# Routing the first half of the tokens inside attention, and the shared expert in two parts, in a transformer block with experts

## The chip, the cores and the metric

The kernel runs on one core of a Trainium2 chip. A core has a matrix engine (PE, or TensorE, with its weight loads shown as PEld), a vector engine (DVE), a scalar engine for activations (ACT), a general engine (POOL, or GpSimd), and an engine that issues transfers (SP). Each engine works off its own instructions in the order written, and waits at semaphores for the others. The metric is the device time of one execution in microseconds (us), as the median of three runs.

## The reference

Four sequences of 1024 tokens with 128 channels pass attention with 16 heads and then a mixture of experts. Cut to what matters:

```
mod = (silu(c) @ wmod).reshape(4, 6, 1, 128)          # sa, ca, ga, sb, cb, gb
h = layernorm(x) * (1 + ca) + sa
x = x + ga * attention(h)                              # causal, rotary, 16 heads of 8 channels
h = layernorm(x) * (1 + cb) + sb
shared = (silu(h @ sg.T) * (h @ su.T)) @ sd.T          # one shared expert, 352 hidden channels
probs = softmax(h @ wr.T + rb)                         # 7 routed experts
w = the two largest probs of a token, divided by their sum
x = x + gb * (shared + sum_e w[e] * expert_e(h))       # each expert like the shared one
```

## The kernel before

**Units.** The 4096 tokens are 32 tiles of 128, and 8 chunks of 512 tokens (CG = 4 tiles each). A half is 4 chunks, 16 tiles, two sequences (GT, GC, GTILES). Attention goes through 16 groups of four heads of one sequence: groups 0 to 3 are sequence 0, groups 12 to 15 sequence 3. NQ is 16, so NQ - 2 and NQ - 1 are the last two.

**Attention.** A group has ten steps of three slots (lines 67 to 71). In a step PE writes two pairs of score matrices (L1681) into banks 0 to 3, ACT takes the exponentials (L973), POOL masks the steps on the diagonal (L775), and PE multiplies the probabilities of two steps earlier with the values (L1658, function `values_product`) into bank 4. The scores of step s, pair p wait for the exponential of the pair before the last. In the slots between, PE works on a ring of three further banks (5 to 7). What goes through it is written out in a list, `RING_PIECES`, made by `quad_pieces`: row maxima of the next groups (L1602 on PE, L1210, L1238, L1243 on DVE), a "shift" that turns these maxima, which ACT and POOL then split in three parts and SP copies into the next group's operands (`load_shift`), a "norm" (PE turns four tiles of output, DVE divides by the sums, L1260 and L1263), and for finished sequences a "turn" (PE transposes, DVE copies, L1249) and a "project" (PE multiplies with the gated output weights L1627, DVE adds to x L1252 and takes statistics L1124). PE writes an entry when DVE, or ACT for a shift, has taken the entry three earlier; DVE works the entries off in the list's order. So both engines follow the same list, and an entry that waits holds up all that is written behind it on PE, the scores included. The slots of turn and project are computed: in group 14 eight entries from slot 9 on, in group 15 four from slot 2 on. The last group writes no maxima.

**Transition.** After group 15, PE transposes and projects the last sequence (L1710, L1766). DVE finishes the variance of sequences 0 to 2 and then of sequence 3; ACT takes the square roots (L995, `deviation`) and normalises chunk by chunk (L1001, `normalise`); PE transposes the rows (L1722, `turn_normalised`), ACT applies the modulation twice (L1011 in full and L1014 as the high part `h2_hi`, `modulate2`), DVE makes the low part (L1293, `second2`). `router` (L1728) gives the logits, and `softmax_shift`, `softmax_scale`, `ranks`, `weights`, `prefix`, `starts`, `slots` and `experts` on DVE make of them each token's two experts and its places in the sorted order; `counts` are two products on PE (L1736). The shared expert of a chunk is three pieces of six products (L1750, `gate_up`), a silu of each (L1030) and a product on DVE (L1416, `hidden`), and twelve products back (L1758, `down`) that DVE adds to x (L1420). A piece is written when the piece two earlier has been taken. All eight chunks pass here, the routing of both halves on DVE between them. POOL modulates the first half's rows (L789, L793) and scatters them with indirect transfers, one per tile and choice, 32 for a half (L782), into `slot_rows_scratch`, which SP has filled with zeros by one transfer of 5.4 MB issued at the end of group 14. The weights of the seven experts come through two raw buffers: SP loads (L617, L618), ACT makes the high part (L1019, `first_part`), DVE the low part (L1425, `second_part`), and the load of expert e waits for the low part of expert e - 2.

**Routed tiles.** Each half has 38 tiles (STG) of 128 sorted rows of one expert. All 76 follow each other as one pipeline: SP loads the rows (L638, four buffers), PE transposes (L1831), ACT and DVE make high and low parts (L1080, L1525), PE multiplies with gate and up weights (L1843), ACT and DVE make the hidden values (L1087, L1532), PE transposes (L1864) and multiplies back (L1854), ACT weighs (L1096), and POOL scatters the result (L844). In the first 24 tiles POOL also has one scatter of the second half's rows in each. SP reads the first half's results back while tiles of the second run, DVE combines them. At the end the second half's results are read, added by POOL (L861) and DVE (L1541, L1543), and stored.

## Time and profile before

| | |
|---|---|
| median of 3 runs | 799.03 us (798.55 to 799.05) |
| profiled execution | 797.6 us, its span 795.9 us |
| mean granted TensorE clock | 0.947 of full speed |
| PE busy | 686.8 us, 86% of the span |
| DVE busy | 573.4 us, 72% |
| ACT busy | 545.9 us, 69% |
| POOL busy | 342.0 us, 43% |
| chain that ended last, by engine | PE 59%, DVE 18%, ACT 9%, issue 7%, DMA 3% |

The span is cut into stages. Attention runs to 489.7, the transition to the first routed tile at 594.7, the tiles to 772, and the rest is reading back and storing. The share of an engine over the whole span is a mean over these, so the stretches below say more. A row of the timeline gives start, duration, engine, line, operation, what is written and read, how many instructions are merged, and in brackets how long the engine had been idle and what ended that. Durations of neighbours overlap a little: the distance of two starts is what an instruction costs on an engine that is full. `PEclk` is the granted clock, 1.00 for 2.4 GHz and 0.50 for 1.2 GHz.

### The profile page before, as it was taken

Reading aid. Unit: us, or ns where it says so; the run is one execution under the profiler, and the core shown is the slowest. Engines: PE = TensorE matmul, PEld = TensorE weight load, DVE = VectorE, ACT = ScalarE, POOL = GpSimd, SP = SyncE. Lnnn points to the kernel's source line nnn. Section 1 sums busy time; section 2 is a strip of 40 time slices with the busy share of each in tenths; the row PEclk is TensorE's granted clock in tenths of the full one; section 3 lists DMA queues with packets and bytes.
Section 4 is the critical chain, followed back from the end, with each engine's and each line's share of the span. In section 5 each row is a group of like instructions: output and inputs, shape, how many; then the busy total and the mean of one; then the engine's idle time right before and its main releaser. Section 6 shows DMA issues by size and latency. Waiting matters only on the chain.

```text
span 795.9 us, 18082 instructions
## 1 busy us (share of the span) xinstructions
PE 686.8 (86%) x5304; PEld 395.3 (50%) x5304; DVE 573.4 (72%) x2042; ACT 545.9 (69%) x1013; POOL 342.0 (43%) x551
## 2 busy tenths in 40 slices
PE   2986899999999999999999986678869989999970
PEld 1553123333333333333333434567659889999960
DVE  5797889999999999999999834574773323333543
ACT  2785259889989888989888788544325556666640
POOL 1367613232322322232322123235657887666652
PEclk9999569999999999999999999699999999999995
DMA  9246021111111111111110079202233322223425
GB/s 260 83 156 219 1 74 47 39 30 29 47 47 48 47 28 30 41 46 47 48 37 14 1 136 178 68 23 81 63 92 78 82 76 81 66 68 104 131 87 158
DMA packets 64760, 59.46 MB, mean 75 GB/s; under 512 B 10798, under 2 KB 52398, under 8 KB 64668
## 3 DMA queue, kind: packets, MB, share of 16 engines
q1 hardware_dynamic: 58924, 46.85, 23.3%
q0 software_dynamic: 4480, 9.64, 3.4%
q10 hardware_dynamic: 1264, 1.84, 0.7%
q8 instruction: 46, 0.75, 0.4%
q14 instruction: 46, 0.38, 0.2%
HBM read 33.57 MB, written 24.33 MB: 73 GB/s over the span
## 4 chain that ended last, share of the span: by engine, by line
PE 59%; DVE 18%; ACT 9%; issue 7%; DMA 3%; POOL 1%; SPq 1%; ACTq 1%; DVEq 0%; POOLq 0%
PE ps L1658 13%; PE ps L1602 10%; PE ps L1843 9%; PE ps L1681 7%; PE ps L1854 6%; DVE junk L1238 5%; ACT probs L973 5%; PE ps L1864 3%; PE ps L1758 2%; PE ps L1636 2%; DVE junk L1210 2%; PE ps L1750 2%; DMA routed_results_scratch<-y_s,s_dest 1%; PE ps L1831 1%; DVE rot L1193 1%
## 5 line engine op out<-in xcount | busy, mean ns | idle before, releaser
L973 ACT ACTIVATE probs<-ps 128x1024 f32<-128x1024 f32 (+1 forms) x320 | 285.5, 941 | 34.5 <-PE ps L1681 32.1
L1210 DVE CUSTOM_DVE_ANT_0 junk<-ps,tri 128x512 f32<-128x512 f32 (+3 forms) x512 | 218.5, 487 | 13.9 <-PE ps L1602 11.6
L1602 PE MATMUL ps<-ka,qa 61*128 61x256 bf16 (+3 forms) x788 | 186.7, 325 | 10.0 <-DVE rowmax L1210 3.0
L775 POOL TENSOR_SCALAR_AFFINE_SELECT probs<-probs 128x512 f32<-128x512 f32 x128 | 79.7, 634 | 191.8 <-ACT probs L973 191.8
L1658 PE MATMUL ps<-probs,v 128*32 128x512 f32 (+3 forms) x1536 | 157.7, 498 | 1.3 <-POOL probs L775 1.1
L1681 PE MATMUL ps<-qa,ka 64*128 64x512 bf16 (+3 forms) x768 | 144.6, 331 | 7.7 <-ACT probs L973 5.6
L1602 PEld LDWEIGHTS ps<-ka,qa 61*128 61x128 bf16 x788 | 53.0, 95 | 159.8 <-DVE rowmax L1210 80.4
L844 POOL DMA_INDIRECT routed_results_scratch<-y_s,s_dest x76 | 76.2, 1003 | 41.0 <-issue 35.0
L782 POOL DMA_INDIRECT slot_rows_scratch<-rows,slot x64 | 64.1, 1001 | 56.6 <-DVE slot L1393 30.1
L1243 DVE TENSOR_REDUCE leftmax<-ps 128x1 f32<-128x512 f32 x120 | 78.4, 686 | 8.5 <-PE ps L1602 8.5
L1532 DVE TENSOR_TENSOR hid_s<-sg,ps 128x352 f32<-128x352 f32 x76 | 39.6, 521 | 46.2 <-ACT sg L1087 46.0
L1854 PE MATMUL ps<-wd,hidT 128*128 (+1 forms) x456 | 64.3, 277 | 5.8 <-ACT hidT L1105 5.8
L1525 DVE TENSOR_TENSOR h_lo<-ps,h_hi 128x128 fp32r<-128x128 f32 x76 | 22.2, 291 | 59.7 <-ACT h_hi L1080 59.3
L1854 PEld LDWEIGHTS ps<-wd,hidT 128*128 128x128 f32 (+1 forms) x456 | 60.6, 192 | 7.4 <-issue 7.3
L1658 PEld LDWEIGHTS ps<-probs,v 128*32 128x32 f32 x1536 | 33.8, 108 | 54.5 <-issue 49.3
L1681 PEld LDWEIGHTS ps<-qa,ka 64*128 64x128 bf16 x768 | 42.5, 94 | 33.4 <-ACT probs L973 21.2
L1087 ACT ACTIVATE sg<-ps 128x352 f32<-128x352 f32 x76 | 35.2, 463 | 33.8 <-PE ps L1843 32.0
L1096 ACT ACTIVATE y_s<-ps,s_weight 128x128 f32<-128x128 f32 x76 | 27.9, 367 | 33.5 <-PE ps L1854 25.4
L1238 DVE CUSTOM_DVE_ANT_0 junk<-ps,above 128x256 f32<-128x256 f32 x136 | 49.3, 419 | 0.0
L749 POOL TENSOR_TENSOR mrest<-mneg,mparts 32x128 f32<-32x128 f32 x16 | 6.7, 417 | 92.7 <-ACT mparts L936 92.7
L1843 PE MATMUL ps<-w_hi,h_hi 128*128 x152 | 45.3, 380 | 1.2 <-issue 1.1
L1210 DVE DVE_READ_ACCUMULATOR2_ANT rowmax<- 128x1 f32 x512 | 42.6, 83 | 0.1
(195 smaller groups left out, 1168.4 us busy)
## 6 DMA issues: line engine op xcount, KB each, us to landing
slot_rows_scratch<-cst SPq DMA_DIRECT2D x1, 5396.0 KB, 36.1
srow<-slot_rows_scratch SPq DMA_DIRECT2D x76, 71.0 KB
k_parts_scratch<-qk_parts SPq DMA_DIRECT2D x12, 320.0 KB, 2.7
ka<-k_parts_scratch SPq DMA_DIRECT2D x32, 120.0 KB
q_parts_scratch<-qk_parts SPq DMA_DIRECT2D x12, 256.0 KB, 2.6
qa<-q_parts_scratch SPq DMA_DIRECT2D x32, 96.0 KB
ka<-k_parts_scratch SPq DMA_DIRECT2D x32, 80.0 KB
xs<-in_x SPq DMA_DIRECT2D x4, 512.0 KB, 9.4
```

What stands on the lines that cost most here:

```text
L775: nc.gpsimd.affine_select(out=p, in_=p, compare_op=ALU.is_ge, fill=0.0, base=0, pattern=[[0, HQ], [1, T]], channel_multiplier=-1).then_inc ...
L782: nc.gpsimd.indirect_dma_start(slot_d, bass.IndirectOffsetOnAxis(ap=slot[:, k, t:t + 1], axis=0), rows[:, t, :], None).then_inc(s_scatter[ ...
L844: nc.gpsimd.indirect_dma_start(y_d, bass.IndirectOffsetOnAxis(ap=s_dest[:, d:d + 1], axis=0), y_s[:, j, :], None).then_inc(s_y_out[j], 16)
L973: nc.scalar.activation(probs[(n * NS + s) % 4][:, 2 * h:2 * h + 2, 0:UNTIL[s] - FROM[s]], ps[:, 2 * h:2 * h + 2, FROM[s]:UNTIL[s]], ACT.Ex ...
L1210: last = V.tensor_tensor_reduce(out=junk[:, bank - 5, at:at + w], in0=ps[:, bank, at:at + w], in1=tri[:, CH - w:CH], scale=1.0, scalar=LOW ...
L1238: last = V.tensor_tensor_reduce(out=junk[:, bank - 5, cols], in0=ps[:, bank, cols], in1=above[:, h, q - CG, :], scale=1.0, scalar=LOW, op0 ...
L1243: last = V.reduce_max(leftmax[m][:, row, q - CG:q - CG + 1], ps[:, bank, :], AX.X)
L1602: last = MM(ps[:, bank, at:at + w], qa[m][g0:g0 + KS, c0 + q * T:c0 + (q + 1) * T], ka[m][g0:g0 + KS, d0 + k0:d0 + k0 + w], start=True, st ...
L1658: last = MM(ps[VW * h:VW * (h + 1), 4, q0:CH], v4[m][:, k, h, :], probs[(n * NS + s) % 4][:, h, p0:p0 + CH - q0], start=begins, stop=ends ...
L1681: last = MM(ps[:, 2 * pair + g, at:at + CH - q0], ka[m][g * HG:(g + 1) * HG, pair * KW + kb * T:pair * KW + (kb + 1) * T], qa[m][g * HG:(g ...
L1843: last = MM(ps[:, 1 + 2 * t2 + g, 0:NI], ht[:, t2, :], wt[:, bass.ds(e, 1), g, :], start=(k == 0), stop=(k == 2))
L1854: last = MM(ps[:, 6, 0:D], hidT[0:w, t2, c, :], wd[0:w, bass.ds(e, 1), c, :], start=(c == 0), stop=(c == len(IC) - 1))
```

## The change

In the last two groups of attention the turns and projections of the first half's chunks are moved to slots 19 to 29 of group 14, written out in a table. DVE then takes the first half's variance, ACT its square root after the exponentials of step 2 of group 15, and DVE normalises these rows itself. Group 15's ring gets, for the four chunks of the half, a "rows" entry (PE transposes, DVE modulates into hT) and a "router" entry (PE multiplies, DVE adds the bias), then turn and project of chunks 4 and 5, and one "counts". The whole choice of experts and slots of the first half runs on DVE between these entries. POOL modulates the first half's rows in steps 5 and 6 of group 15. ACT has `deviation(0)` and `exp7(0)` in that group.

In the transition PE transposes the already modulated rows of chunks 0 to 3, ACT copies them once and DVE makes the low part; only these four chunks pass the shared expert there, along with the rows and routers of chunks 4 to 7. Then come the 38 tiles of the first half, with the routing and row modulation of the second half as thirteen portions on DVE, one per tile; the shared expert of chunks 4 to 7; and the 38 tiles of the second half. POOL's scatters of the second half stand 11 in the last 11 tiles of the first half and 21 behind them. SP reads the first half's results before it waits for these scatters. Some buffers in SBUF change places: the shared expert's are no longer shared with the routed tiles' own.

```
+FIRST_HALF = [(19, "turn", 0), (20, "turn", 1), (21, "project", 0), (23, "turn", 2), (24, "project", 1),
...
+SECOND_HALF = [(9, "rows", 0), (10, "rows", 1), (11, "router", 0), (12, "rows", 2), (13, "router", 1), (14, "rows", 3),
...
 (POOL)
+                    for u in range(GC) if n == NQ - 1 else ():
+                        if s == (ROWS_TURNED[u] // SLOTS) + 2:
+                            modulate_rows(u)
...
-                pool.wait_ge(s_hid, len(IC) + 1 + x // 2)
                 scatter(k, t)
...
+                if g == 0 and STG - ALONG <= s < STG:
+                    scatter_second(s - STG + ALONG)
+            pool.wait_ge(s_expert, 1)
+            slot_steps(0, -2, 3, slot_step)
+            for x in range(ALONG, TOP * GT):
+                scatter_second(x)
+            pool.wait_ge(s_expert, GRP)
+            slot_steps(1, -2, 3, slot_step)
 (ACT)
+                    if s == 2 and n == NQ - 1:
+                        deviation(0)
+                    if s == 7 and n == NQ - 1:
+                        exp7(0)
...
             for u in range(2):
                 act.wait_ge(s_ot, u + 1)
                 nc.scalar.activation(oT[:, u, :], ps[:, u, :], ACT.Copy).then_inc(s_oT, 1)
-            normalise(1)
...
+            for n in range(GC):
+                modulate2(n)
             deviation(1)
+            silu(0)
             normalise(4)
...
+            slot_steps(0, -1, 2, slot_step)
+            for n in range(GC, NC):
+                silu(n)
+            slot_steps(1, -1, 2, slot_step)
 (DVE)
+                if done == ("project", NQ - 2, None, GC - 1):
+                    variance(GTILES[0], s_var2)
+                    scale2(0)
+                    dve.wait_ge(s_v4, NQ)
+                    for n in range(GC):
+                        normalise(n)
+                elif done == ("router", NQ - 1, None, GC - 1):
+                    V.memset(beats[:], 0.0).then_inc(s_beats, 1)
+                    softmax_shift(0)
+                elif done == ("project", NQ - 1, None, GC):
+                    softmax_scale(0)
+                    dve.wait_ge(s_beats, 1)
+                    beaten(0, range(NE))
+                elif done == ("project", NQ - 1, None, GC + 1):
+                    ranks(0)
+                    weights(0)
...
+                if g == 0 and s >= 1:
+                    next(routing, None)
 (PE)
+            pe.wait_ge(s_expert, 1)
             pe.wait_ge(s_wd, 16 * len(IC))
             pe.wait_ge(s_wlo, NE)
-            pe.wait_ge(s_shared, NC)
+            pe.wait_ge(s_shared, GC)
...
+            slot_steps(0, -1, 2, slot_step)
+            pe.wait_ge(s_shid, STG)
+            for n in range(GC, NC):
+                gate_up(n)
+                if n > GC:
+                    down(n - 1)
+            down(NC - 1)
+            pe.wait_ge(s_expert, GRP)
+            pe.wait_ge(s_shared, NC)
+            slot_steps(1, -1, 2, slot_step)
```

**On PE, step 3 of group 15.** Before, between the scores of step 3 (`ps<-qa,ka`) stands nothing, and one norm (`ps<-eye,outT`) follows in step 4:

```order
L1681 MATMUL ps<-qa,ka 128x512 [waits s_exp]
L1681 MATMUL ps<-qa,ka 128x512
L1681 MATMUL ps<-qa,ka 128x512 [waits s_exp]
L1681 MATMUL ps<-qa,ka 128x512
L1658 MATMUL ps<-probs,v_0 32x256 [waits s_mask,s_exp]
L1658 MATMUL ps<-probs,v_0 32x256 x3
L1681 MATMUL ps<-qa,ka 128x512 [waits s_exp]
L1681 MATMUL ps<-qa,ka 128x512
L1636 MATMUL ps<-eye,outT 128x128 [waits s_outT,s_ring_free]
```

Now the transpositions of normalised rows (`ps<-eye,rows`) and the first router product (`ps<-wr,hT`) stand between them:

```order
L1702 MATMUL ps<-qa,ka 128x512 [waits s_exp]
L1702 MATMUL ps<-qa,ka 128x512
L1642 MATMUL ps<-eye,rows 128x128 [waits s_xn2,s_ring_free]
L1642 MATMUL ps<-eye,rows 128x128 x3
L1702 MATMUL ps<-qa,ka 128x512 [waits s_exp]
L1702 MATMUL ps<-qa,ka 128x512
L1642 MATMUL ps<-eye,rows 128x128 [waits s_xn2,s_ring_free]
L1642 MATMUL ps<-eye,rows 128x128 x3
L1679 MATMUL ps<-probs,v_0 32x256 [waits s_mask,s_exp]
L1679 MATMUL ps<-probs,v_0 32x256 x3
L1646 MATMUL ps<-wr,hT 128x7 [waits s_ring_free]
L1646 MATMUL ps<-wr,hT 128x7 x3
```

The second scores of step 3 have moved behind a wait for DVE's normalised rows (`s_xn2`).

**On PE, the end of group 15.** Before, the last value products follow the last scores:

```order
L1681 MATMUL ps<-qa,ka 128x384 [waits s_exp]
L1681 MATMUL ps<-qa,ka 128x384
L1681 MATMUL ps<-qa,ka 128x128 x2
L1658 MATMUL ps<-probs,v_0 32x512 [waits s_exp]
L1658 MATMUL ps<-probs,v_0 32x512 x3
```

Now the counts (`ps<-sel,cst`) stand ahead of them:

```order
L1702 MATMUL ps<-qa,ka 128x384 [waits s_exp]
L1702 MATMUL ps<-qa,ka 128x384
L1702 MATMUL ps<-qa,ka 128x128 x2
L1613 MATMUL ps<-sel,cst 128x112 [waits s_sel,s_ring_free]
L1613 MATMUL ps<-sel,cst 128x112
L1679 MATMUL ps<-probs,v_0 32x512 [waits s_exp]
L1679 MATMUL ps<-probs,v_0 32x512 x3
```

The last three value products of attention have moved behind a wait for the choice of experts on DVE (`s_sel`).

**On DVE, the end of attention.** Before, the last normalisation of output follows the variance of three sequences:

```order
L1138 SCALAR_TENSOR_TENSOR rstd<-part_a,part_b 128x24 [waits s_link]
L1148 RECIPROCAL rstd<-rstd 128x24 [waits s_std2]
L1149 SCALAR_TENSOR_TENSOR nbias<-mean,rstd 128x24 [waits s_link]
L1260 RECIPROCAL recip<-ps 128x16 [waits s_ring,s_ring_free]
L1263 TENSOR_TENSOR xn<-ps,recip 128x4x32 [waits s_link]
```

Now it follows the slots and experts of the first half (the last rows of a run of 36 that begins with the counts' result):

```order
L1364 TENSOR_REDUCE slot_f<-chosen 128x16 [waits s_link]
L1365 CAST slot<-slot_f 128x16 [waits s_link]
L1369 TENSOR_TENSOR passed<-cst,tend 1x266
L1371 TENSOR_REDUCE expert_f<-passed 1x38 [waits s_link]
L1372 TENSOR_SCALAR expert<-expert_f 1x38 [waits s_link]
L1245 RECIPROCAL recip<-ps 128x16 [waits s_ring]
L1248 TENSOR_TENSOR xn<-ps,recip 128x4x32 [waits s_link]
```

The routing of the first half has moved from the transition to a place ahead of attention's last normalisation.

## Rows read from the trace of the kernel before

**Rows 1.** Four stretches: us, busy time (x instructions) by engine, granted clock, DMA, GB/s.

```profile
463.40:485.00 21.60, 19.86 (x184) 7.94 (x184) 6.57 (x23) 18.56 (x23) 4.29 (x7) 1.00 1.10 195
...
485.00:489.70 4.70, 2.13 (x25) 0.92 (x20) 1.03 (x4) 3.57 (x7) 1.22 (x2) 1.00 1.18 150
489.70:594.70 105.00, 79.95 (x464) 67.26 (x464) 69.33 (x203) 47.35 (x85) 49.85 (x48) 0.90 0.29 73
594.70:772.00 177.30, 168.79 (x1216) 162.18 (x1216) 69.08 (x164) 108.14 (x379) 126.68 (x252) 0.98 0.31 87
```

**Rows 2.** Timeline, start of group 15: PE's first scores, ACT's exponentials of step 2.

```profile
463.48 0.61 PE L1681 MATMUL ps<-qa,ka 64*128 64x512 bf16 x4 [1.68 <-DMA qa<-mparts]
...
467.81 1.94 ACT L973 ACTIVATE probs<-ps 128x1024 f32<-128x1024 f32 x2
```

**Rows 3.** Timeline, end of attention: ACT and DVE.

```profile
484.98 1.28 ACT L995 ACT_TABLE_LOAD   x1
486.28 0.22 ACT L995 ACTIVATE rstd<-rstd 128x24 f32<-128x24 f32 x1
...
489.40 0.29 DVE L1263 TENSOR_TENSOR xn<-ps,recip 128x128 f32<-128x128 f32 x1
```

**Rows 4.** Timeline of ACT: copies h_hi of routed tiles 0, 25, 59 and 75.

```profile
595.32 0.28 ACT L1080 ACTIVATE h_hi<-ps 128x128 fp32r<-128x128 f32 x1 [3.76 <-PE ps L1831]
...
656.06 0.27 ACT L1080 ACTIVATE h_hi<-ps 128x128 fp32r<-128x128 f32 x1
...
729.05 0.28 ACT L1080 ACTIVATE h_hi<-ps 128x128 fp32r<-128x128 f32 x1
...
764.57 0.28 ACT L1080 ACTIVATE h_hi<-ps 128x128 fp32r<-128x128 f32 x1
```

**Rows 5.** Timeline of PE: a projection; third pieces of chunks 2 and 3; router, transpositions.

```profile
473.77 1.16 PE L1627 MATMUL ps<-wo_gated,oT 128*128 128x128 f32 x8
...
535.16 0.48 PE L1750 MATMUL ps<-h_hi,ws_hi 128*96 128x512 f32 x1 [2.29 <-DVE hid L1416]
...
539.30 0.96 PE L1728 MATMUL ps<-wr,hT 128*128 128x7 f32 x8
540.12 0.63 PE L1722 MATMUL ps<-eye,rows 128*128 128x128 f32 x4
...
545.81 0.47 PE L1750 MATMUL ps<-h_hi,ws_hi 128*96 128x512 f32 x1 [2.28 <-DVE hid L1416]
```

**Rows 6.** The line of the first normalisation: duration min/median/max in ns, first and last start.

```profile
L1165 DVE TENSOR_SCALAR xn<-xs,mean,rstd x8: 341/343/345, 10.1 to 11.9; 128x128 f32<-128x128 f32 x8
```

**Rows 7.** Timeline of DVE: the first half's routing, ends of its two runs.

```profile
509.88 0.26 DVE L1318 TENSOR_REDUCE rsum<-prob 128x16 f32<-128x112 f32 x1
...
514.48 0.22 DVE L1338 TENSOR_SCALAR sel<-rank 128x112 f32<-128x112 f32 x1
...
519.21 0.27 DVE L1355 COPY tot<-ps 128x112 f32<-128x112 f32 x1 [1.92 <-PE ps L1736]
...
529.01 0.17 DVE L1400 TENSOR_SCALAR expert<-expert_f 1x38 int32<-1x38 f32 x1
```

**Rows 8.** A stretch inside the transition, columns as in rows 1.

```profile
499.00:502.00 3.00, 2.63 (x14) 2.56 (x14) 0.19 (x1) 1.21 (x3) 2.39 (x3) 0.50 1.02 231
```

**Rows 9.** Timeline: load of the last expert's raw weights, and its split on DVE.

```profile
586.59 0.33 SPq L617 DMA_DIRECT2D w_raw<-in_gate  x1
...
591.60 0.89 DVE L1425 TENSOR_TENSOR w_lo<-w_raw,w_hi 128x704 fp32r<-128x704 f32 x1 [0.75 <-ACT w_hi L1019]
```

**Rows 10.** Timeline of POOL: a scatter of rows, two and the last of results.

```profile
532.26 0.95 POOL L782 DMA_INDIRECT slot_rows_scratch<-rows,slot  x1 [0.30 <-issue]
...
634.90 1.00 POOL L844 DMA_INDIRECT routed_results_scratch<-y_s,s_dest  x1 [0.16 <-issue]
...
637.66 1.00 POOL L844 DMA_INDIRECT routed_results_scratch<-y_s,s_dest  x1 [0.16 <-issue]
...
773.21 0.96 POOL L844 DMA_INDIRECT routed_results_scratch<-y_s,s_dest  x1 [1.05 <-issue]
```

476 lines of the change are left out of this document (218 added, 258 removed).

## The prediction

> **What bounds the kernel now.** I read the page's totals and slices first, then the stretches [rows 1], then the rows at their borders. The last attention group (463.4 to 485.0) is shared between PE (19.9 of 21.6 us busy) and ACT (18.6). Then come 4.7 us with PE half empty, and 105 us of transition (489.7 to 594.7) in which PE is busy 80, DVE 69, ACT 47 and no engine is full. The routed tiles (594.7 to 772) are PE's: 169 of 177 us. So a transition whose engines wait for each other stands between two stages that are nearly full, and work put into these costs its own length.
>
> Below, T is the start of the last group, E the end of the last normalisation of attention output, H0, H37, H38, H75 the starts of ACT's h_hi copy for tiles 0, 37, 38 and 75. In the kernel before T is 463.5 [rows 2], E 489.7 [rows 3], H0 595.3 and H75 764.6 [rows 4]. Its ledger: 463.5 + 26.2 (to E) + 105.6 (to H0) + 169.3 (to H75) + 31.3 (to the end of the span) = 795.9.
>
> **Group 14: T comes earlier, 1.8 us.** PE waited 1.68 us for the shift rows [rows 2]. The shift now has two turns at 0.6 and a projection at 1.1 [rows 5] fewer ahead of it, 2.2 us. Behind it PE has 8.4 us of work where 8.0 passed before, which covers the shift's way over ACT, POOL and DMA. T = 463.5 - 2.2 + 0.4 = 461.7; bounds are 0 and 4 earlier.
>
> **Group 15: E - T grows from 26.2 to 44.8.** All times in this part are counted from T.
> - ACT finishes step 2 at 6.3, as before (469.75) [rows 2]. Now a table load of 1.28 and the square root of 0.22 stand there [rows 3]: 7.8. DVE needs 0.6 for reciprocal and bias, then four normalisations at 0.26 (eight of them start between 10.1 and 11.9 in [rows 6]): 9.6. PE stands at the first transposition of rows from 5.6 on, so it loses 4.0. Behind it wait the second scores of step 3, and ACT. DVE's other twelve normalisations, 3.1 us, come ahead of the first modulation, and the first router product waits 1.5 more.
> - From there PE sets the pace. In the group before, its last scores start at about 19.7, with some 1.7 idle (21.6 less 19.9) [rows 1]. Added are 4 transpositions at 0.6 and 4 routers at 0.82 [rows 5], 5.7 us; turns and projections are two and two before and after. Last scores: 19.7 - 1.7 + 5.7 + waits of 4.0, 1.5 and 1.9 in small pieces (ACT's second table load among them) = 31.1. The exponentials of step 7 end some 3.2 earlier, at 27.9.
> - The choice of experts starts there: exponential 0.3 on ACT; on DVE, from scale to choice, 509.88 to 514.70 less a memset of 0.75 = 4.1 [rows 7]; between them in its queue one normalisation of output 0.6 and a projection with its statistics 1.5; with the steps from engine to engine 34.7. PE's counts wait for it from 31.4 on, and behind them the last three value products, which before ran at once: 3.3 us lost.
> - The counts take 0.7, DVE's weights end at 36.0. Then prefix, starts, slots and experts, 519.21 to 529.18 less three hidden products at 0.6 [rows 7]: 8.1, to 44.1. The last normalisation is queued behind them, though PE has its input ready at 40.0: E = 44.8. Before, all this lay in the transition.
>
> E would be 461.7 + 44.8 = 506.5. I add 1.5 for PE's clock: it was granted 0.50, the lower of its two levels, in 499 to 502 [rows 8], after the 4.7 us in which PE was busy 2.1 [rows 1], and the group now has two such gaps. E = 508.0, 18.3 later. Bounds for the clock: 0 and 12.
>
> The trace shows ACT's load of 1.28 and the square root 1.30 after the load's start, with no gap before the load [rows 3]. The Trainium skill ("ScalarE: Activation LUTs", What ACT_TABLE_LOAD costs) gives the same 1283 ns for a load but about 1380 ns of drain with it. By the page the two switches inside the group would cost 2.8 us more; here the trace does not agree, and the sum goes by it.
>
> **Transition, first half only: H0 - E falls from 105.6 to 62.5.** Times counted from E.
> - The first shared product starts at 6.6: output transpositions 1.1, ACT's copies 1.9 up to the first subtraction at 3.0, then two subtractions and two additions with statistics on DVE.
> - The first hidden product waits for deviation and silu, with a table load each on ACT, until 12.7. The next chunk starts at 17.2, once normalise(4) is through.
> - A chunk took 10.65 us (535.16 to 545.81): PE's own 8.4 and a wait of 2.28 for the first hidden product [rows 5], which stands behind modulate, normalise and a weight copy on ACT. That order on ACT is unchanged (a weight copy less in chunk 1, one more in chunk 3), so chunks start at 17.2, 27.3 and 38.0, and PE is through at 53.
> - The tiles also wait for all seven experts' weights. The loads of 5 and 6 go out when DVE has split 3 and 4, at 52.7 and 56.1. A load up to the end of its split takes 586.59 to 592.49 = 5.9 [rows 9]: 61.9. Before, four further chunks covered this. Transposition and copy add 0.6: H0 = E + 62.5 = 570.5.
> - The 32 scatters are queued on POOL at 1.25 each [rows 10] from E - 2.7 on and are through by E + 39: not late.
>
> Bounds for this stretch: 42.5 (scatters alone) and 70.
>
> **First 38 tiles: H37 - H0 = 83.0.** Undisturbed tiles come every 2.15 us (34 of them in 656.06 to 729.05 [rows 4]), 79.5 for 37. DVE has 2.15 - 0.8 = 1.3 us free in a tile, and the routing of the second half comes in thirteen portions; prefix 1.9, starts 2.0 and slots 3.1 are longer. Their excess of 3.1, less some slack in the hand-over, costs 2.5. POOL with both scatters in a tile needs 2.77 (634.90 to 637.66) [rows 10]; before, this cost PE 7.0 us (60.7 for the first 25 tiles, less 25 x 2.15) [rows 4], after 9 tiles of lag had been absorbed. Now there are only 11 such tiles: 1.0. H37 = 653.5.
>
> **Between the halves: H38 - H37 = 43.8, of which any two tiles have 2.15.** PE: 7.0 to drain (three tile lengths and a little), then 12 pieces at 1.4 and 4 down products at 2.7, 27.6, plus 2 in short waits, plus 0.4: 37.0. POOL: its lag of 11 x 0.62 stands, so its last y scatter ends 13.5 after H37 (8.6 undisturbed, 773.21 - 764.57 [rows 4, 10]); 21 scatters at 1.25 follow, the last starts at 38.7 and lands 2.2 later; row load and first transposition 2.9: 43.8. SP reads the first half's results in this gap, not ahead of a tile. Bounds 37 and 50. H38 = 697.3.
>
> **Second 38 tiles and end.** 79.5, so H75 = 776.8. The end is as before, 31.3: 808.1. Against 795.9 that is +12.2: to E +18.3, transition -43.1, tiles and gap (83.0 + 43.8 + 79.5 against 169.3) +37.0. The profiled execution took 797.6, 1.7 over its span; the median of the runs is 799.0, 1.4 above it. Forecast: 799.0 + 12.2 = 811.2, so 811.
>
> **Rivals.**
> 1. Faster: the first half of the transition runs up to its scatters. For: half of the shared work, routing and row modulation have left DVE and ACT, which were busy only 69 and 47 of 105 us [rows 1]. If chunks come at PE's 8.4 and the splits keep up, H0 = E + 42.5, 20 us earlier: 791. It decides for faster once more than 12.2 of the 20 come. Against: the wait of 2.28 hangs on ACT's order, which stays, and two buffers for raw weights tie each load to a split.
> 2. The two late waits do not come: splits are done when PE is (-8.6), and POOL catches up so that the gap is PE's 37.0 (-6.8): 796. Against: the order of the splits, and 2.77 us per tile.
> 3. Slower still: after the stall of 4 us at the first rows, PE's clock stays at half for the some 12 us of full work that follow: +12, 823. For: 0.50 at 499 to 502 [rows 8]. Against: PE's work there is dense, and the group before was granted 1.00 [rows 1]. The Trainium skill ("TensorE: Matmul & The Clock Gate", HAM oscillation) describes such re-throttling between bursts; this trace shows it around the transition, not in attention's full groups.
>
> **How the numbers follow.** The forecast has 0.64, with its own range 803 to 819 (4 us of doubt in each of attention, transition and gap); each rival has 0.12. Within 0.2% (1.6 us), about what this measurement can tell from no change, lies a third of rival 2: 0.04. Faster: rival 1, half of rival 2 and a little of the forecast's edge, 0.20. Slower: 0.76. The range leaves out most of rival 1 and the upper edge of rival 3: 796 to 822.
>
> **What would show it.** Right: an ACT table load after the exponentials of step 2, PE idle 4 us before its first transposition of rows; PE idle 3 us before the counts, and the last normalisation 43 to 47 us after T; the first tile released by a weight split; tile 38 released by a scatter and its row load, PE idle some 6 us before it. Wrong: E less than 12 us later, H0 less than 50 after E, or the second half's tiles started by PE's own down product.

## The result and the profile after

The kernel after the change takes 821.8 us (median of 4 runs, 819.9 to 821.9) against 798.8 for the kernel before in the same session: 1.0284 times as long, with a 95% interval of 1.0266 to 1.0302. The forecast was 811 with a range of 796 to 822. Slower was right; the size was half of what came (12.2 us forecast, 23.0 measured), and the time lies only 0.2 us inside the upper end of the range. The profiled execution took 819.9, its span is 817.9. The ledger of the forecast, filled in from the new trace (the marks stand as defined there):

| stretch, us | before | forecast | after | miss |
|---|---|---|---|---|
| start to T (group 15 begins) | 463.5 | 461.7 | 460.4 | -1.3 |
| T to E (last normalisation of output) | 26.2 | 46.3 | 53.0 | +6.7 |
| E to H0 (first routed tile) | 105.6 | 62.5 | 63.4 | +0.9 |
| H0 to H37 | | 83.0 | 85.0 | +2.0 |
| H37 to H38 | | 43.8 | 45.3 | +1.5 |
| H38 to H75 | | 79.5 | 79.5 | 0 |
| H0 to H75 together | 169.3 | 206.3 | 209.8 | +3.5 |
| H75 to the end | 31.3 | 31.3 | 31.3 | 0 |
| span | 795.9 | 808.1 | 817.9 | +9.8 |

The marks are rows of the timeline of the kernel after: PE's first scores of group 15, DVE's last normalisation, and ACT's copies h_hi of tiles 0, 37, 38 and 75 (they answer to [rows 2 to 4]).

```profile
460.42 0.61 PE L1702 MATMUL ps<-qa,ka 64*128 64x512 bf16 x4
...
513.08 0.29 DVE L1248 TENSOR_TENSOR xn<-ps,recip 128x128 f32<-128x128 f32 x1
...
576.74 0.28 ACT L1048 ACTIVATE h_hi<-ps 128x128 fp32r<-128x128 f32 x1 [1.61 <-PE ps L1821]
...
661.78 0.28 ACT L1048 ACTIVATE h_hi<-ps 128x128 fp32r<-128x128 f32 x1
...
707.04 0.28 ACT L1048 ACTIVATE h_hi<-ps 128x128 fp32r<-128x128 f32 x1 [13.63 <-PE ps L1821]
...
786.55 0.28 ACT L1048 ACTIVATE h_hi<-ps 128x128 fp32r<-128x128 f32 x1
```

Where PE stands, in the timeline of PE (idle time and what ended it in brackets): at the first rows, at the first router, before the counts, behind the last normalisation, before tile 0 and before tile 38.

```profile
470.12 1.03 PE L1642 MATMUL ps<-eye,rows 128*128 128x128 f32 x4 [3.73 <-DVE rows L1402]
...
477.68 1.84 PE L1646 MATMUL ps<-wr,hT 128*128 128x7 f32 x8 [3.94 <-DVE hT L1229]
...
503.14 0.67 PE L1613 MATMUL ps<-sel,cst 128*128 128x112 f32 x4 [2.45 <-DVE sel L1309]
...
513.43 1.97 PE L1731 MATMUL ps<-eye,xn 128*128 128x128 f32 x8 [3.77 <-DVE xn L1248]
...
576.25 0.44 PE L1821 MATMUL ps<-eye,srow 128*128 128x128 f32 x1 [7.54 <-DVE w_lo L1397]
...
706.56 0.45 PE L1821 MATMUL ps<-eye,srow 128*128 128x128 f32 x1 [7.31 <-DMA srow<-slot_rows_scratch]
```

Five of the six waits were forecast, in their places and about in size (4.0, 3.3, 4.8, 8.6 and 6.8 us; all but the last are 0.3 to 1.1 shorter than that). The one at the first router was put at 1.5 and is 3.94. The transpositions of rows take 1.03 for four, where [rows 5] had 0.63. Both are seen in the windows of the kernel after (columns as in [rows 1]):

```profile
470.00:474.00 4.00, 3.62 (x18) 1.68 (x18) 4.00 (x9) 1.57 (x2) 2.49 (x2) 0.57 1.17 175
474.00:477.00 3.00, 0.00 (x0) 0.00 (x0) 3.00 (x5) 0.00 (x0) 2.55 (x3) 1.00 1.11 162
477.00:487.30 10.30, 9.62 (x50) 6.76 (x50) 3.03 (x8) 2.65 (x3) 2.36 (x2) 0.50 1.14 176
```

TensorE's clock is at its lower level in most of the first stretch and in all of the third, and PE is busy 3.62 and 9.62 us there. In the second, DVE is busy all the time with five instructions, priced at 0.26 each in the forecast. The lines of the normalisations, in the kernel before (eight of them, [rows 6]), had at most 345 ns. In the kernel after (duration in ns min/median/max, first and last start):

```profile
L1402 DVE TENSOR_SCALAR rows<-xs,mean,rstd x16: 333/340/1284, 468.9 to 475.5; 128x128 f32<-128x128 f32 x16
```

### The profile page after: what moved, and what is told of

Its sections match the earlier page's. It is cut to its first block and busy times, and to the rows that moved or that the text cites. A ratio compares the mean times of both kernels' runs of the same rounds, so it can differ in the third digit from the quotient of the medians.

```text
span 817.9 us, 17963 instructions
## 1 busy us (share of the span) xinstructions
PE 695.4 (85%) x5320; PEld 399.4 (49%) x5320; DVE 584.0 (71%) x2062; ACT 539.4 (66%) x994; POOL 342.4 (42%) x550
## 5 line engine op out<-in xcount | busy, mean ns | idle before, releaser
L1182 DVE CUSTOM_DVE_ANT_0 junk<-ps,tri 128x512 f32<-128x512 f32 (+3 forms) x512 | 218.4, 487 | 13.6 <-PE ps L1605 11.4
L1679 PE MATMUL ps<-probs,v 128*32 128x512 f32 (+3 forms) x1536 | 160.5, 507 | 0.3 <-ACT outT L943 0.3
L1605 PEld LDWEIGHTS ps<-ka,qa 61*128 61x128 bf16 x788 | 52.9, 95 | 159.7 <-DVE rowmax L1182 79.4
L780 POOL DMA_INDIRECT slot_rows_scratch<-rows,slot x64 | 61.7, 964 | 27.5 <-issue 18.9
L1526 DVE TENSOR_TENSOR hid_s<-sg,ps 128x352 f32<-128x352 f32 x76 | 39.6, 521 | 46.6 <-ACT sg L1055 46.6
L1844 PE MATMUL ps<-wd,hidT 128*128 (+1 forms) x456 | 63.6, 275 | 3.5 <-ACT hidT L1073 3.5
L1702 PEld LDWEIGHTS ps<-qa,ka 64*128 64x128 bf16 x768 | 42.5, 94 | 31.3 <-ACT probs L955 22.2
## 6 DMA issues: line engine op xcount, KB each, us to landing
xs<-in_x SPq DMA_DIRECT2D x4, 512.0 KB, 10.3
```

Source lines behind the costliest of these rows:

```text
L780: nc.gpsimd.indirect_dma_start(slot_d, bass.IndirectOffsetOnAxis(ap=slot[:, k, t:t + 1], axis=0), rows[:, t, :], None).then_inc(s_scatter[ ...
L1182: last = V.tensor_tensor_reduce(out=junk[:, bank - 5, at:at + w], in0=ps[:, bank, at:at + w], in1=tri[:, CH - w:CH], scale=1.0, scalar=LOW ...
L1605: last = MM(ps[:, bank, at:at + w], qa[m][g0:g0 + KS, c0 + q * T:c0 + (q + 1) * T], ka[m][g0:g0 + KS, d0 + k0:d0 + k0 + w], start=True, st ...
L1679: last = MM(ps[VW * h:VW * (h + 1), 4, q0:CH], v4[m][:, k, h, :], probs[(n * NS + s) % 4][:, h, p0:p0 + CH - q0], start=begins, stop=ends ...
L1702: last = MM(ps[:, 2 * pair + g, at:at + CH - q0], ka[m][g * HG:(g + 1) * HG, pair * KW + kb * T:pair * KW + (kb + 1) * T], qa[m][g * HG:(g ...
L1844: last = MM(ps[:, 6, 0:D], hidT[0:w, t2, c, :], wd[0:w, bass.ds(e, 1), c, :], start=(c == 0), stop=(c == len(IC) - 1))
```

## The experiments

Each is the kernel after with the edit shown. Time is the median with the lowest and highest execution; the ratio is to the kernel before on the same chip, with its 95% interval; the stretches are from the profiled execution. Weights, portions and along17 leave group 15 as it is in the kernel after, and their 52.9, 53.3 and 54.3 show how far T to E moves by itself. T does too: it lies between 460.4 and 462.3 in kernels that are the same up to there, so the -1.3 in the ledger's first row is no finding.

| kernel | time, us | ratio | T to E | E to H0 | H0 to H37 | H37 to H38 |
|---|---|---|---|---|---|---|
| after | 821.8 (819.9-821.9) | 1.0284 [1.0266, 1.0302] | 53.0 | 63.4 | 85.0 | 45.3 |
| pool_late | 813.2 (809.7-819.6) | 1.0198 [1.0152, 1.0243] | 44.9 | 65.2 | 84.7 | 45.1 |
| fill | 815.4 (814.6-816.2) | 1.0213 [1.0187, 1.0239] | 48.7 | 63.9 | 85.1 | 44.9 |
| norm_first | 817.2 (814.1-819.8) | 1.0224 [1.0197, 1.0250] | 50.2 | 62.9 | 85.1 | 44.9 |
| order | 818.9 (817.7-819.9) | 1.0253 [1.0240, 1.0266] | 49.3 | 63.7 | 85.2 | 44.8 |
| order_late | 814.6 (813.2-815.5) | 1.0194 [1.0180, 1.0207] | 46.5 | 63.4 | 85.2 | 44.8 |
| weights | 813.4 (809.7-814.2) | 1.0190 [1.0163, 1.0216] | 52.9 | 53.2 | 85.1 | 44.9 |
| portions | 818.6 (816.7-820.1) | 1.0246 [1.0231, 1.0262] | 53.3 | 63.6 | 82.2 | 44.9 |
| along17 | 818.5 (816.8-819.9) | 1.0249 [1.0221, 1.0278] | 54.3 | 62.2 | 87.7 | 42.2 |
| combo | 801.3 (799.1-802.1) | 1.0024 [1.0014, 1.0034] | 46.6 | 53.1 | 82.4 | 44.8 |
| three | 804.4 (798.5-808.8) | 1.0061 [1.0032, 1.0089] | 52.9 | 53.4 | 82.1 | 45.0 |
| tuned | 797.5 (791.4-801.7) | 0.9982 [0.9957, 1.0006] | 39.1 | 53.3 | 82.0 | 44.9 |
| steady (other chip, see its text) | 844.7 (843.9-846.0) | 1.0143 [1.0124, 1.0161] | 39.0 | 75.5 | 93.3 | 62.0 |

**pool_late: POOL beside DVE.**

```
-                pool.wait_ge(s_ring, RING_INDEX["rows", NQ - 1, None, n] + 1)
+                pool.wait_ge(s_ring, max(RING_INDEX["rows", NQ - 1, None, n],
+                                         RING_INDEX["router", NQ - 1, None, 0]) + 1)
```

> Only change to the kernel after: POOL starts the row modulation of chunk n once PE has written the first router product (and the rows of chunk n), instead of as soon as the rows are turned, so that it no longer runs beside DVE's 16 normalisations. Theory A (DVE's one-source operation and POOL's two-source operation take turns: while POOL modulates, from 471.3 on, DVE does 2 normalisations in 1.3 us where it did one per 0.26): the 16 normalisations take 4.3 us instead of 7.96, PE's wait before the first router product falls from 3.9 to under 0.8, and the time by 3.6, to 818.2; if TensorE's clock then also stays at its upper level in the following 10 us, by up to 5 more, to 813. Theory B (DVE was slowed by the transfer of 5.4 MB that runs in the same stretch at 1.1 of the DMA engines): the 16 take 8 us as before, 821.8. Theory C (it goes, but the choice of experts later in the group takes the gain back): normalisations 4.3 us, time within 1 us of 821.8.

Theory A. The timeline of pool_late, DVE's 16 normalisations, PE's first router and POOL's first modulation:

```profile
469.07 4.20 DVE L1402 TENSOR_SCALAR rows<-xs,mean,rstd 128x128 f32<-128x128 f32 x16 [0.15 <-DVE nbias L1120]
...
474.13 1.03 PE L1646 MATMUL ps<-wr,hT 128*128 128x7 f32 x8 [0.19 <-DVE hT L1229]
...
475.34 1.19 POOL L744 TENSOR_TENSOR rows<-rows,mod_rows 128x512 f32<-128x512 f32 x1 [7.06 <-PE ps L1646]
```

and of the kernel after:

```profile
468.86 7.96 DVE L1402 TENSOR_SCALAR rows<-xs,mean,rstd 128x128 f32<-128x128 f32 x16 [0.15 <-DVE nbias L1120]
...
471.33 1.30 POOL L744 TENSOR_TENSOR rows<-rows,mod_rows 128x512 f32<-128x512 f32 x1 [3.26 <-PE ps L1642]
```

4.20 us instead of 7.96 with the transfer of 5.4 MB still running beside them, so that rival is out. The wait at the first router is gone (0.19). T to E fell by 8.1: 3.8 are the normalisations, and the rest goes with the clock, which in this execution was low for 3.4 us up to PE's wait before the counts, where the kernel after had 3.4 and 10.3. This edit doesn't hold the clock still, so that share is read from the windows and not isolated. T to E is now 44.9; the forecast, without its 1.5 for the clock, had 44.8. E to H0 gave 1.8 back (65.2): from 518 to 523, in the first chunks of the shared expert, the granted clock was 0.66, where the kernel after had 1.00 at that place.

**fill: the clock.** A helper writes the unit matrix, transposed, into the ring's bank; it is called ahead of two waits.

```
+            def filler(bank, times):
+                for k in range(times):
+                    nc.tensor.transpose(ps[:, bank, k % CG * T:(k % CG + 1) * T], eye[:], eye[:])
...
+                    if what == 0:
+                        filler(bank, 24)
                     pe.wait_ge(s_xn2, what + 1)
...
+                    if what == 0:
+                        filler(bank, 32)
                     ring_taken(pe, RING_INDEX["rows", n, None, what])
```

> Only change to the kernel after: PE transposes the unit matrix 24 times (3.6 us at the upper clock) into the ring's bank ahead of its wait for the first normalised rows, and 32 times (4.9 us) ahead of its wait for the first modulated rows. These products are thrown away; they stand where PE otherwise waits 3.7 and 3.9 us. Theory A (the two gaps bring TensorE's clock to its lower level in 470 to 474 and 477 to 487, and this, not only the gaps themselves, makes the last group longer): the granted clock of these stretches is 1.00, the transpositions of rows take 0.6 instead of 1.1, the last normalisation of attention comes 5 to 6.5 us earlier, time 816. Theory B (the clock is at half, but in this group ACT or DVE sets the pace, so the clock costs nothing): time 821.8 plus 0 to 1. Theory C (the clock falls there for another reason than the gaps): clock 0.5 in the same stretches, time 821.8 or up to 3 more.

Theory A, at two thirds of its size. The window of fill over 470.2 to 494.0:

```profile
470.20:494.00 23.80, 22.01 (x182) 14.69 (x182) 16.06 (x36) 9.55 (x12) 10.40 (x9) 1.00 0.99 179
```

The upper level throughout, and E comes 4.1 earlier though the waits themselves are still there (PE only works through them). So the lower clock in this stretch was worth 4.1 us of the 53.0, give or take the 1.4 by which T to E moves by itself. The clock fell later instead, before the counts (0.50 over 498.4 to 502.4, where the kernel after had 1.00; the mean from T to E is 0.92 against 0.82), so what the upper level all the way to E would bring is not shown.

**norm_first: the last normalisation ahead of the slots.** The slots are cut behind their totals; the normalisation is taken there, and then comes the rest.

```
-                    slots(0, incl, bank)
+                    late = slots(0, incl, bank)
+                    next(late)
                     dve.sem_inc(s_ring_free, 1)
-                    experts(0, end)
+                    rest.extend((late, end))
...
+            for _ in rest[0]:
+                pass
+            experts(0, rest[1])
```

> Only change to the kernel after: DVE takes the last normalisation of output after the totals of the first half's slots and before the slots themselves and experts (3.4 us of its work), which then run while ACT and PE work on the last projection. Theory A (PE stood 3.8 us because this normalisation was queued behind the routing): it comes 2.9 us earlier, PE's wait there falls to 0.8 to 1, the rest follows, time 819. Theory B (the first shared products wait for the subtractions that now come behind slots and experts): the first shared product as late as before, 821.8.

Theory A: T to E is 2.8 shorter, PE's wait there 0.90 instead of 3.77, H0 2.8 earlier. In its timeline of PE:

```profile
511.12 1.37 PE L1739 MATMUL ps<-eye,xn 128*128 128x128 f32 x8 [0.90 <-DVE xn L1249]
```

The median moved by 4.6, more than the trace accounts for; the executions lie 5.7 apart.

**order and order_late: another order of the ring.**

```
-SECOND_HALF = [(9, "rows", 0), (10, "rows", 1), (11, "router", 0), ...
-               (15, "router", 2), (16, "router", 3), (17, "turn", 4), (18, "turn", 5), (20, "project", 4), ...
+SECOND_HALF = [(3, "turn", 4), (4, "turn", 5), (6, "project", 4), (8, "project", 5), (11, "rows", 0), (12, "rows", 1),
+               (13, "router", 0), (13, "rows", 2), (14, "router", 1), (15, "rows", 3), (15, "router", 2), ...
```

> Change to the kernel after, in the ring of group 15 alone: the turns and projections of chunks 4 and 5 come first (slots 3, 4, 6, 8), then the rows and routers of the first half (slots 11 to 16), the counts stay in slot 28. DVE takes its wait for ACT's square root and the 16 normalisations after the projection of chunk 5, the whole choice of experts in one piece after the norm of step 7; ACT takes exp7 after step 6. No work is added or taken away. Theory A (the group was long because PE stood at waits and ran at the lower clock behind them): the waits of 3.7 and 3.9 us at the rows and the first router and that of 2.5 before the counts go to under 1 each, the clock stays at 1.00 through the group, the distance from the group's start to the last normalisation falls from 53.0 to 39 to 42 us, time 808 to 811. Theory B (the added work itself is what fills the group): distance 48 to 51, time 818 to 820. Theory C (the earlier last normalisation only exposes the next wait, scatters or weights): distance 39 to 42, but the first tile comes less than 4 us earlier, 818 to 821.

> The kernel 'order', and POOL's row modulation of each chunk waits for the first router product, as in 'pool_late'. Theory A (DVE and POOL only hurt each other while the normalisations run, and in this order nothing on PE stands close behind them): 16 normalisations 4.2 us instead of 6 to 8, time 0 to 3 less than 'order'. Theory B (the contention is the larger part of what 'pool_late' gained): time 4 or more less than 'order'.

Neither theory of order holds as put. Its distance, 49.3, and its time are B's, but not because PE's work fills the group: PE is busy 33.9 of these 49.3 us. The waits moved. Counted from T, DVE came to its normalisations 2.0 us later (472.24 against 468.86, with T 1.4 later), behind two projections, and POOL was beside them again. In order's timeline:

```profile
472.24 7.96 DVE L1402 TENSOR_SCALAR rows<-xs,mean,rstd 128x128 f32<-128x128 f32 x16 [0.15 <-DVE nbias L1120]
...
473.51 0.63 PE L1642 MATMUL ps<-eye,rows 128*128 128x128 f32 x4 [2.30 <-DVE rows L1402]
...
481.07 1.84 PE L1646 MATMUL ps<-wr,hT 128*128 128x7 f32 x8 [5.27 <-DVE hT L1229]
...
511.18 1.97 PE L1731 MATMUL ps<-eye,xn 128*128 128x128 f32 x8 [5.47 <-DVE xn L1248]
```

The wait before the counts did go to 0.57, and came back behind the last normalisation (5.47), since DVE's 8 us of slots stand between. The four waits add up to 13.6 us, and in the kernel after to 13.9. The clock, which theory A had at 1.00 throughout, was low as well.

Order_late removes the contention (its 16 normalisations take 4.19, PE's wait at the first router 1.50). Its median is 4.2 us under order's, which is theory B by little; T to E is 2.8 shorter, and the profiled executions differ by 3.1, which is theory A. In the other order the same edit gave 8.6 and 8.1, so it is worth less here. The clock is part of that, as this window of order_late shows:

```profile
479.90:491.90 12.00, 12.00 (x64) 7.05 (x56) 1.98 (x7) 3.92 (x6) 6.13 (x7) 0.50 1.14 171
```

For 12 us PE was busy all the time and had the lower level, where pool_late at that place had the upper one.

**weights: the experts' weights.** ACT's and DVE's copies go two at a time into the gaps before chunks 5, 6 and 7.

```
             silu(1)
+            first_part(0)
+            first_part(1)
             modulate2(5)
...
             second2(4)
+            second_part(0)
+            second_part(1)
             hidden(2, 0)
```

> Only change to the kernel after: ACT makes the high parts of the seven experts' weights two at a time in the first three of its gaps before a modulation (experts 0 and 1 before chunk 5, 2 and 3 before chunk 6, 4 and 5 before chunk 7, 6 after it), DVE their low parts right after the low part of the chunk before, so that the last load goes out about 9 us earlier. Theory A (the tiles wait 7.5 us for the last split, as the forecast said): the first routed tile starts 5 to 6 us earlier relative to attention's end (63.4 falls to 58), time 816. Theory B (something else, rows scattered by POOL or the routers, is ready just as late): first tile less than 2 us earlier, 820 to 822. Theory C (the copies now delay silu or modulation, and each chunk takes longer): chunk starts move from 10.6 apart to 11.5 or more, and the gain is half, 819.

Theory A and more: E to H0 is 10.2 shorter. In its timeline of PE, the third pieces of chunks 2 and 3 and the first tile:

```profile
544.63 0.47 PE L1764 MATMUL ps<-h_hi,ws_hi 128*96 128x512 f32 x1 [1.58 <-DVE hid L1388]
...
554.58 0.47 PE L1764 MATMUL ps<-h_hi,ws_hi 128*96 128x512 f32 x1 [1.58 <-DVE hid L1388]
...
566.14 0.45 PE L1821 MATMUL ps<-eye,srow 128*128 128x128 f32 x1 [2.44 <-DVE w_lo L1397]
```

The same pieces in the kernel after:

```profile
545.16 0.64 PE L1764 MATMUL ps<-h_hi,ws_hi 128*96 128x512 f32 x1 [2.25 <-DVE hid L1388]
...
558.04 0.47 PE L1764 MATMUL ps<-h_hi,ws_hi 128*96 128x512 f32 x1 [2.94 <-DVE hid L1388]
```

The wait before tile 0 fell from 7.54 to 2.44. The chunks are 9.95 apart, where these two were 12.88 apart and the pair before 10.6. Both distances together are 3.6 us: low parts no longer stand between DVE's hidden products nor high parts ahead of silu. The wait gives 5.1, and the last 1.5 lie behind these pieces.

**portions: DVE's routing in the tiles.** prefix, starts, slots, beaten and the modulations are cut into 23 portions by `yield`, and the counts of the second half come at step 10 instead of 7.

> Only change to the kernel after: DVE's routing of the second half is cut into 23 portions of at most 1.3 us, one per tile, instead of 13 of up to 3.1; PE's counts for it come 3 tiles later. Theory A (the long portions prefix, starts and slots hold up three tiles by 1.1 us each, and beaten and the modulations some tiles by 0.2): the distance from tile 0 to tile 37 falls from 85.0 to 80.5 to 82, and since POOL's queue sets the start of tile 38 and starts its scatters with tile 27, tile 38 comes as much earlier; time 818. Theory B (the long portions are absorbed and the lost time is from the clock at the tiles' start): distance 84 to 85, time 821.8.

Theory A: H0 to H37 is 82.2 instead of 85.0, and H38 follows. ACT's copies h_hi show where the 5.5 us above 79.5 lay in the kernel after. This is its tile 16:

```profile
616.80 0.28 ACT L1048 ACTIVATE h_hi<-ps 128x128 fp32r<-128x128 f32 x1
```

Tile 0 started at 576.74, so the first 16 tiles, in which DVE's portions run, took 40.1 us where 16 x 2.15 is 34.4. The next 21, with POOL's 11 scatters at their end, took 45.0 against 45.2. With the portions cut up, the 16 take 36.0, and those up to tile 25, into which the portions now reach, are 2.7 over in all. A start at the lower clock is not what remains: the second half's tiles start at it too, behind a wait as long, and its first 16 take 34.2. In the kernel after:

```profile
707.04:711.04 4.00, 2.93 (x10) 2.60 (x11) 0.58 (x2) 0.88 (x3) 1.57 (x10) 0.50 0.21 55
```

So DVE's routing cost up to 5.5 us, of which the cut gave back 2.8; tiles of the first half without any routing were not run.

**along17: POOL's scatters.**

```
-        ALONG = 11
+        ALONG = 17
```

> Only change to the kernel after: 17 instead of 11 of the 32 scatters of the second half's rows stand in the last tiles of the first half (one in each), 15 behind them. Theory A (POOL's queue sets the start of tile 38; a tile with one scatter leaves POOL 0.65 idle, so 6 more tiles with two let it finish 3.9 earlier; PE's tiles of the first half end 2 to 4 later since POOL's lag now passes what the buffers hold, but PE is not the one that is waited for between the halves): the distance from tile 0 to tile 38 falls from 130.3 to 126.5, PE's idle time before tile 38 from 7.3 to 0 to 2; time 818. Theory B (PE loses in the tiles what the gap gives back): distance 129 to 131, time 821 to 823. Theory C (two indirect transfers per tile slow each other so that every tile with two costs 2.77 for all engines): distance longer by 4, 825.

Theory B in the trace: from tile 0 to tile 38 it is 129.9 against 130.3. PE's wait before tile 38 falls from 7.3 to 0.8, so POOL's queue was what tile 38 waited for; but the 37 tiles grow by 2.7, all of it behind tile 25. Its timeline of PE, a down product near the end of the first half and tile 38:

```profile
669.75 0.93 PE L1844 MATMUL ps<-wd,hidT 128*128 x6 [1.41 <-ACT hidT L1073]
...
706.55 0.30 PE L1821 MATMUL ps<-eye,srow 128*128 128x128 f32 x1 [0.83 <-issue]
```

The times (818.5 against 821.8, in different sessions) overlap in their intervals, so a gain of some 3 us is neither shown nor excluded.

**combo, three and tuned: together.** Combo is order_late with weights and portions; three is pool_late with weights and portions, in the kernel's own order. Tuned is three, with the turns of chunks 4 and 5 in slots 7 and 8, their projections in 17 and 18, exp7 after step 6, 14 filler transpositions ahead of the first rows, the choice of experts in one piece, and norm_first.

> The kernel 'order_late' with the edits of 'weights' and 'portions'. Theory A (the losses are separate and add up, and none of them is a price of the change itself): 821.8 less 12 for the order and POOL, less 8 to 10 for the weights, less 3.5 for the portions gives 797 to 799, level with the kernel before. Theory B (behind attention something not yet seen is next: the scatters of the first half, which end 41 us after they start, or the copies on ACT): first tile 58 or more after attention's end, time 803 or more. Theory C (the parts help each other, as a shorter wait also keeps the clock up): under 796.

> The kernel after with the edits of 'pool_late', 'weights' and 'portions' together, and its own order of the ring. Theory A (the three losses are separate; each was measured alone at 8.0 us before the last normalisation, 10.3 between it and the first tile, 2.8 in the tiles): attention's last normalisation 44.9 us after the group's start, first tile 53 behind it, 82.3 from tile 0 to 37; the span is 817.9 less 21.1 = 796.8, the time 799 by this kernel's usual distance, level with the kernel before (798.9). Theory B ('combo' at 801.3 was held by a limit that all share, and not by its own order of the ring): 801 again.

> 'three', and in group 15: the turns of chunks 4 and 5 go in slots 7 and 8, ahead of the wait for rows, with 14 thrown-away transpositions of the unit matrix behind them; their projections in 17 and 18; exp7 after step 6; the choice of experts in one piece after the norm of step 7; and DVE takes the last normalisation of output between the totals and the slots of the first half, so that slots and experts run while ACT and PE turn the last rows. Theory A (each shortens a wait of PE seen in 'pool_late': 3.7 at the rows to 0.5, which also keeps the clock up, 2.5 before the counts to under 1, 2.6 behind the last norm to 0.6): the distance from the group's start to the last normalisation 37 to 40 instead of 44.9, time 792 to 795, faster than the kernel before. Theory B (the group is then filled by PE's work and ACT's exponentials, as in 'order' the waits only move): distance 42 to 45, time 797 to 800.

Combo: the three gains add up in the trace (46.6, 53.1, 82.4), and it ends 0.24% above the kernel before, between its theories A and B. Three: its stretches behind attention are as expected, but its profiled execution, which is its slowest (808.8), has 52.9 from T to E, where pool_late had 44.9 with the same instructions in attention and the same wait at the first rows (3.74 and 3.73 us). The windows over the same stretch, first of pool_late, then of three, then of tuned:

```profile
470.20:494.00 23.80, 21.39 (x166) 12.15 (x166) 16.39 (x55) 13.15 (x16) 10.64 (x10) 0.93 1.00 173
```

```profile
470.20:494.00 23.80, 21.93 (x106) 13.87 (x106) 10.67 (x32) 8.48 (x9) 9.37 (x8) 0.51 1.11 181
```

```profile
470.20:494.00 23.80, 20.64 (x174) 11.73 (x178) 17.12 (x62) 13.30 (x16) 11.52 (x12) 1.00 0.98 175
```

In three, TensorE was at its lower level for nearly all of these 23.8 us (0.51), in pool_late for 3.4 of them. In three the level fell during the wait at the first rows (0.89 over 469 to 470, then 0.50), in pool_late at its end (1.00 over 469 to 470, 0.72 over the next us). PE was busy as long in both, but with 106 instructions in the one and 166 in the other. T to E differs by 8.0 us, for the same instructions. Three's twelve executions lie in groups, five at 798.5 to 800.9, two at 804, five at 808.4 to 808.8, the last with the lowest clock (0.924 to 0.926 over the span). Tuned spreads from 791.4 to 801.7, with clocks from 0.949 to 0.934. Its profiled execution (792.5) bears theory A out (T to E 39.1), its median of 797.5 theory B; against the kernel before (798.96) it is not faster by what this can tell.

**steady: all waits of the group filled.** Tuned with 20, 12 and 20 filler transpositions at three waits.

> 'tuned' with more thrown-away transpositions of the unit matrix, so that PE hardly stands in the last group: 20 instead of 14 ahead of the first rows (0.4 us left of a wait of 1.1), 12 ahead of the first router product (a wait of 1.6), and 20 ahead of the wait for the last normalisation of output (2.6). 'tuned' lay between 791.4 and 801.7 over its executions, with a granted clock of 0.949 to 0.934, and its profiled one (792.5) had the upper level in the whole group. Theory A (the spread is the clock's answer to these short waits, which is not the same in every execution, and filled waits leave it nothing to answer to, as 'fill' with all its executions within 1.7 us suggests): all executions within 3 us, clock 0.945 or more, median 790.5 to 793, faster than the kernel before by 0.7 to 1.0%. Theory B (the spread has its cause elsewhere, in the waits of the transition or in the chip): 791 to 802 again, median 796 to 798.

This gives no verdict on the time. It ran on a chip on which the kernel before took 833.6 us instead of 799, and where steady took 844.7 (843.9 to 846.0). Its executions lie 2.1 us apart, as theory A had it, but with a clock of 0.920 to 0.926 and not 0.945. T to E is 39.0 there with the upper clock from 470.2 to 494.0, as in tuned. What is long is the transition, the tiles of the first half and the gap (75.5, 93.3 and 62.0). Its window over that stretch of attention, and a row of its timeline of PE in the transition:

```profile
470.20:494.00 23.80, 21.72 (x185) 13.20 (x185) 17.19 (x60) 14.37 (x17) 10.66 (x10) 1.00 1.07 184
```

```profile
528.56 0.74 PE L1792 MATMUL ps<-h_hi,ws_hi 128*96 128x512 f32 x1 [7.11 <-issue]
```

Idle time put down to issue is not above 0.7 us in the transition of the other traces. Whether filled waits make the spread go away on a chip like the others stays open.

## Why the prediction was right, and where it was off

**Sign and places.** T to E grew because work was put between stages that are full, the transition fell by almost what was forecast (to 63.4, forecast 62.5), and the gap between the halves was POOL's and not PE's. The first tile was released by a weight's low part, tile 38 by a row load behind the last scatter, PE was idle 3.7 before the rows and 2.5 before the counts: these signs are in the trace. One that the forecast named is not: the last normalisation was to come 43 to 47 us after T, and came after 53.0. Rival 1 (transition up to its scatters) did not come, though weights shows that half of its 20 us was to be had by moving two kinds of copies. Rival 2 failed on both waits (7.5 and 7.3 us). That the time stayed inside the range is in part luck: 0.2 us more would have left it.

**The step that was mis-sized is T to E**, by 6.7 of the 9.8 us. Two terms of it:
- "DVE's other twelve normalisations, 3.1 us, come ahead of the first modulation, and the first router product waits 1.5 more." The price of 0.26 was read from [rows 6], where POOL is not at work on SBUF. Here POOL modulates the rows that DVE has just made, and the twelve take 6.8. The wait was 3.94. The change's own diff says that POOL starts there; I had priced each engine alone. pool_late shows it: with POOL later, the wait is 0.19, so without POOL even the 1.5 was too much.
- "I add 1.5 for PE's clock." The bounds were 0 and 12. fill puts it at 4.1 in one stretch, and three and pool_late, with the same instructions, lie 8.0 apart. Rival 3 (12 us at half clock behind the first rows, 823) had the mechanism; in the trace the long stretch at the lower level follows the second wait, the one that I had too small, and lasts 10.3 us. Its time of 823 was nearer than the forecast's, but it put 12 us on the clock, and what the runs show is 4.1 and a difference of 8.0.

pool_late has 44.9 where the rest of the chain was put at 44.8, but this agreement is partly luck. Its waits at the first rows, at the router, before the counts and behind the last normalisation are 3.7, 0.2, 2.5 and 2.6, where the forecast had 4.0, 1.5, 3.3 and 4.8, and its clock was still low for some 11 us of that stretch (mean 0.88), which 44.8 has not. That E includes the last normalisation's place behind the slots is shown by norm_first.

**The transition** was right step by step: chunks 1 to 3 start 16.6, 26.5 and 38.7 us after E (forecast 17.2, 27.3 and 38.0), PE is through at 55.3 (53), and the tiles then wait 7.5 for the weights (8.6), so that part of the errors cancel.

**The tiles** are 2.0 over, and here too terms were wrong and partly cancelled. DVE's portions cost up to 5.5 us and not 2.5, as the first 16 tiles show, and POOL's 11 scatters cost the tiles nothing where 1.0 was put. **The gap** is 1.5 over, with its cause right. POOL's last scatter starts 40.3 after H37 instead of 38.7, above all because its scatters of results end 14.7 after H37 and not 13.5. The forecast's own terms, 8.6 and 11 x 0.62, give 15.4 already for the start of the last of them; what brought that down to 13.5 is not told.

**The net.** Undone one at a time, POOL beside DVE, the order of the weights and the long portions give 8.6, 8.4 and 3.2 us, which is 20.2 of the 23.0. Together the same three edits (three) give 17.4 by the median, and from 13 to 23 over its executions; combo, which also has another order of the ring, gives 20.5. So most of what the change cost lay in waits that it made. That the move brings nothing by itself is not shown: with the three taken out the time is about the old one, but PE still waits in group 15 and in the gap of 45 us, and tuned, which shortens the former, reached 791.4 in its fastest execution.

## What to carry to other kernels

When work moves from a half empty stage into a full one, price each instruction beside the engines that will then run with it, not by its row from an empty stretch: two engines that read and write the same memory can take turns instruction by instruction. Count the lower TensorE clock behind every new wait as a cost of its own, with a range, because it is not the same from one execution to the next; ask for several executions before you call a gain of a per cent. And when a stage is halved, look at what its other half was covering: here the loads of the experts' weights.

## What the runs showed of the hardware

- DVE instructions with one input in SBUF (128x128 float32, 0.34 us) and POOL instructions with two (128x512, 1.2 to 1.3 us) took turns: single ones of DVE's lasted up to 1.284 us, and 16 took 7.96 us instead of 4.20, twice (after, order). The Trainium skill ("SBUF — State Buffer", Who interferes with whom) states that the pair of ports that the two share is an exclusive lock, held for the whole instruction; the trace agrees, and POOL lost little (1.30 against 1.19).
- Around one and the same wait of 3.7 us the granted clock fell; it was low for 3.4 us in one execution and for 23.9 in another, with PE busy 21.9 of 23.8 us in the latter (pool_late, three). T to E differed by 8.0 us, 1% of the kernel. In order_late it was 0.50 for 12 us with PE busy all of them. What decides it stays open.
- ACT's switch of tables cost 1.28 us and no more, also inside a full group, as in the timeline of the kernel after:

```profile
466.70 1.28 ACT L931 ACT_TABLE_LOAD   x1
468.00 0.21 ACT L931 ACTIVATE rstd<-rstd 128x16 f32<-128x16 f32 x1
468.23 1.28 ACT L955 ACT_TABLE_LOAD   x1
469.52 1.02 ACT L955 ACTIVATE probs<-ps 128x1024 f32<-128x1024 f32 x1
```

- Chips differ. The kernel before had medians of 798.8 to 799.0 in four sessions, three of them known to be on three different chips, and 833.6 in the fifth, on yet another.
